# Softmax sums moved between on-chip buffers in two halves per sequence, and normalisation on GpSimd, in a fused attention and mixture-of-experts kernel

## What is computed

```python
q = layernorm(x) @ Wq.T + bq            # 32 heads of 16
k = ctx @ Wk.T + bk; v = ctx @ Wv.T + bv    # 8 groups of 16
w = softmax(mask(q k^T / 4))            # [b, group, head in group, query, key]
out = (w @ v) -> [b, 256, 512]
x = x + tanh(g_xattn) * (out @ Wo.T + bo)
xt = layernorm(x)
scores = sigmoid(xt @ gate.T); top 2 of 8 experts, chosen with expert_bias
x = x + tanh(g_ffn) * (routed experts (bf16) + shared expert (f32))
```

## Time and profile before

| | |
|---|---|
| median of three runs | 863.16 us |
| profiled execution | 858.97 us |
| its span, first to last instruction | 856.9 us |
| PE busy | 693.1 us (81%) |
| DVE busy | 469.0 us (55%) |
| ACT busy | 291.4 us (34%) |
| POOL busy | 68.7 us (8%) |
| mean granted TensorE clock | 0.877 of full |

### The profile page before, as it was taken

One profiled execution on the slowest core, in us unless ns is written; L12 is line 12 of the kernel. 1 busy time (PEld: TensorE's weight loads), 2 busy tenths in 40 slices (PEclk: granted clock), 3 DMA queues, 4 the chain that ended last, 5 costly groups with the idle time before them and its releaser, 6 DMA issues. The chain is left out here.

```text
span 856.9 us, 14813 instructions
## 1 busy us (share of the span) xinstructions
PE 693.1 (81%) x4417; PEld 480.3 (56%) x4417; DVE 469.0 (55%) x1041; ACT 291.4 (34%) x601; POOL 68.7 (8%) x100
## 2 busy tenths in 40 slices
PE   0436999699599789869959969989637799999998
PEld 0335758477377568648737747657326344444443
DVE  4417665368458467555836846564223455555554
ACT  1121454244333344433524433443201333333332
POOL 7400001001001000100100100000102000000000
PEclk9965979789799989978979988859657899999999
DMA  4785464444535543553545462430236022222111
GB/s 149 171 228 103 109 159 125 80 103 138 113 97 119 130 100 102 147 86 85 155 81 119 118 129 49 103 84 26 90 74 111 25 62 62 62 62 62 49 48 50
DMA packets 65199, 84.84 MB, mean 99 GB/s; under 512 B 15176, under 2 KB 43664, under 8 KB 64912
## 3 DMA queue, kind: packets, MB, share of 16 engines
q1 hardware_dynamic: 61008, 77.58, 36.9%
q0 software_dynamic: 2304, 6.29, 3.9%
q10 hardware_dynamic: 1856, 0.57, 0.3%
HBM read 60.75 MB, written 29.70 MB: 106 GB/s over the span
## 5 line engine op out<-in xcount | busy, mean ns | idle before, releaser
L593 ACT ACTIVATE probs<-ps 128x512 f32<-128x512 f32 x256 | 147.2, 598 | 150.3 <-PE ps L936 149.9
L800 DVE TENSOR_REDUCE mx<-ps 128x2 f32<-128x512 f32 x256 | 172.6, 683 | 39.7 <-PE ps L917 39.3
L917 PE MATMUL ps<-kst,qst 65*128 65x256 f32 x512 | 127.9, 336 | 65.3 <-DVE mx L800 59.6
L917 PEld LDWEIGHTS ps<-kst,qst 65*128 65x128 f32 x512 | 96.4, 213 | 115.1 <-DVE mx L800 76.1
L1085 PE MATMUL ps_h<-w,q_sg 128*128 128x512 bf16 x512 | 132.8, 383 | 5.2 <-PEq L77 5.2
L936 PE MATMUL ps<-qst,kst 66*128 66x512 f32 x256 | 113.8, 447 | 2.3 <-ACT probs L593 1.1
L1136 DVE SCALAR_TENSOR_TENSOR hid<-ps_h,sc_in,up 128x256 bf16<-128x256 f32 x128 | 61.9, 484 | 87.1 <-ACT up L1126 86.1
L1126 ACT ACTIVATE up<-ps_h,sc_in 128x256 f32<-128x256 f32 x128 | 60.7, 475 | 120.1 <-PE ps_h L1085 120.1
L1085 PEld LDWEIGHTS ps_h<-w,q_sg 128*128 128x128 bf16 x512 | 49.9, 99 | 67.8 <-issue 10.5
L949 PE MATMUL psa<-probs,v_st 128*32 128x256 f32 x1024 | 77.9, 427 | 1.2 <-ACT probs L593 1.2
L1103 PE MATMUL ps_o<-probs,hidT 128*128 128x512 bf16 x256 | 76.2, 380 | 0.8 <-DVE hidT L1142 0.8
(11 more groups left out here) (126 smaller groups left out, 1071.7 us busy)
## 6 DMA issues: line engine op xcount, KB each, us to landing
qst<-q_d SPq DMA_DIRECT2D x96, 128.0 KB
q_d<-q_sg SPq DMA_DIRECT2D x32, 256.0 KB, 3.0
a_d<-a_sb SPq DMA_DIRECT2D x32, 256.0 KB, 2.2
x_n<-in_x SPq DMA_DIRECT2D x8, 512.0 KB, 4.0
c_raw<-in_ctxT SPq DMA_DIRECT2D x8, 512.0 KB, 3.4
w<-in_w13T POOLq DMA_DIRECT2D x8, 512.0 KB, 16.1
x<-in_x SPq DMA_DIRECT2D x8, 512.0 KB, 3.4
a_dn<-a_d SPq DMA_DIRECT2D x8, 512.0 KB
```

The costliest lines, as they stand in the source:

```text
L593: act.activation(probs[:, v % 8, :], ps2[v % 2][:, :, :].rearrange("p h q -> p (h q)"), ACT.Exp, scale=HD ** -0.5).then_inc(s_exp, 1)
L800: dve.tensor_reduce(mx[:, c % 2, 0:8 * NT].rearrange("p (h t) -> p h t", t=NT)[:, h:h + 2, w // 2], ps1[u % 2][:, :, :], AX_X, ALU.max)\
L917: last = pe.matmul(o[:, i, :], qst[0:ROW_MAX, c, h, t * P:t * P + P], kst[0:ROW_MAX, c, g % 2, :], start=(i == 0 or not masked), stop=not ...
```

## The change

Four things change for each sequence:

1. The sums no longer go through DRAM on their way to `den`. `move_sums(b, c)` copies the rows of a chunk's sums straight from `a_sb` to 32 rows of `den`, in two DMAs, just ahead of `store_a` of the same chunk (u = 24, 1, 8, 17).
2. Values, reciprocal and its store and load are done in two halves of two chunks each. Half 0: values loaded and reciprocal stored at u = 5 (DVE's reciprocal at u = 4), loaded back at u = 9. Half 1: values loaded at u = 20, DVE's reciprocal at u = 20, stored at u = 21, loaded back at u = 23, which is behind `load_stack(b+1, 0)`.
3. The multiplication and the low part move from DVE to POOL, in halves by chunk, 128x512 each (`normalise`, `low_values`). ACT's high copies are at u = 16 and 27. POOL's order becomes values 2, power, normalise 0, low 0, values 3, residual and bias, values of b+1, normalise 1, low 1, powers, values.
4. W0 waits for both halves of the low part.

```diff
-            def load_sums(b):
-                for i in range(2):
-                    ready((s_aw[i], b * 32 + 32))
-                sp.dma_start(den[:, :], a_d[b, :, HD, :]).then_inc(s_den, 16)
-                sp.dma_start(a_dn[:, :, :].rearrange("p c q -> p (c q)"), a_d[b, :, 0:HD, :]).then_inc(s_ar, 16)
...
+            def move_sums(b, c):
+                ready((s_aev, b * G + 2 * c + 2), (s_rd, b * 2 + c // 2 - 1))
+                for w in range(2):
+                    row = 32 * c + 16 * w
+                    sp.dma_start(den[row:row + 16, :], a_sb[HD:P:32, c % 2, w, :]).then_inc(s_den[c % 2], 16)
+
+            def load_values(b, h):
+                for i in range(2):
+                    ready((s_aw[i], b * 32 + 16 * h + 16))
+                ready((s_ln2, b * LN2))
+                sp.dma_start(a_dn[:, 2 * h:2 * h + 2, :].rearrange("p c q -> p (c q)"),
+                             a_d[b, :, 0:HD, 2 * L * h:2 * L * h + 2 * L]).then_inc(s_ar[h], 16)
+
+            def store_r(b, h):
+                ready((s_rd, b * 2 + h + 1))
+                for i in range(2):
+                    c = 2 * h + i
+                    sp.dma_start(r_d[b, h, :, L * i:L * i + L], rden[32 * c:32 * c + 32, :]).then_inc(s_rw, 16)
+
+            def load_r(b, h):
+                ready((s_rw, b * 64 + 32 * h + 32), (s_ln2, b * LN2))
+                sp.dma_start(f(a_lo[:, 2 * h:2 * h + 2, :].rearrange("p c q -> p (c q)")),
+                             r_d[b, h].unsqueeze(1).broadcast_to([G, HD, 2 * L])).then_inc(s_rr[h], 16)
...
                     if prev and u in (1, 8, 17):
-                        store_a(b - 1, {1: 1, 8: 2, 17: 3}[u])
+                        c = {1: 1, 8: 2, 17: 3}[u]
+                        move_sums(b - 1, c)
+                        store_a(b - 1, c)
...
-                    if u == 18 and prev:
-                        load_sums(b - 1)
+                    if prev and u in (5, 20):
+                        load_values(b - 1, u // 20)
+                    if prev and u in (5, 21):
+                        store_r(b - 1, u // 21)
+                    if prev and u in (9, 23):
+                        load_r(b - 1, u // 23)
...
-                    if u == 21 and prev:
-                        store_r(b - 1)
...
-                    if u == 22 and prev:
-                        load_r(b - 1)
...
                     if attn and u == 24:
+                        move_sums(b, 0)
                         store_a(b, 0)
...
+            def normalise(b, h):
+                pool.wait_ge(s_rr[h], b * 16 + 16)
+                pool.wait_ge(s_ar[h], b * 16 + 16)
+                half = a_dn[:, 2 * h:2 * h + 2, :]
+                pool.tensor_tensor(half, half, a_lo[:, 2 * h:2 * h + 2, :].bitcast(F32), ALU.mult).then_inc(s_an, 1)
+
+            def low_values(b, h):
+                pool.wait_ge(s_ahi, b * 2 + h + 1)
+                pool.tensor_tensor(a_lo[:, 2 * h:2 * h + 2, :], a_dn[:, 2 * h:2 * h + 2, :],
+                                   a_hi[:, 2 * h:2 * h + 2, :].bitcast(F32), ALU.subtract).then_inc(s_alo, 1)
...
+                if attn:
+                    values(b, 2, None)
                 if nxt:
                     deviation1(b + 1)
+                if prev:
+                    normalise(b - 1, 0)
+                    low_values(b - 1, 0)
                 if attn:
-                    values(b, 2, None)
+                    values(b, 3, None)
                 if prev:
                     residual_bias(b - 1)
-                if attn:
-                    values(b, 3, None)
                 if nxt:
                     values(b + 1, 0, idx)
                 if prev:
+                    normalise(b - 1, 1)
+                    low_values(b - 1, 1)
                     deviation2(b - 1, 0)
...
-                    if u in (27, 28) and prev:
-                        t = u - 27
-                        act.wait_ge(s_an, b * NT - NT + t + 1)
-                        act.activation(a_hi[:, :, t * P:t * P + P], a_dn[:, :, t * P:t * P + P], ACT.Copy)\
+                    if u in (16, 27) and prev:
+                        h = u // 27
+                        act.wait_ge(s_an, b * 2 - 2 + h + 1)
+                        act.activation(a_hi[:, 2 * h:2 * h + 2, :], a_dn[:, 2 * h:2 * h + 2, :], ACT.Copy)\
                             .then_inc(s_ahi, 1)
...
-                    if u == 21 and prev:
-                        dve.wait_ge(s_den, b * 16)
-                        dve.reciprocal(rden[:, :], den[:, :]).then_inc(s_rd, 1)
-                    if u in (26, 27) and prev:
...
+                    if u in (4, 20) and prev:
+                        h = u // 20
+                        for i in range(2):
+                            dve.wait_ge(s_den[i], b * 64 - 64 + 32 * h + 32)
+                        wait(dve, s_rw, b * 64 - 128 + 32 * h + 32)
+                        dve.reciprocal(rden[64 * h:64 * h + 64, :], den[64 * h:64 * h + 64, :]).then_inc(s_rd, 1)
...
-                    pe.wait_ge(s_alo, b * NT + k + 1)
+                    pe.wait_ge(s_alo, b * 2 + 2)
```

More of the change, by code:

```diff
@@ L91, in attention_phase @@
         a_d = dram("a_d", (B, G, 32, CH * L))
-        r_d = dram("r_d", (B, G, CH * L))
+        r_d = dram("r_d", (B, 2, G, 2 * L))
         def pair(name, cols):
@@ L206, in attention_phase @@
         s_aw = [sem(f"s_aw{i}") for i in range(2)]
-        s_den = sem("s_den")
+        s_den = [sem(f"s_den{i}") for i in range(2)]
         s_rd = sem("s_rd")
         s_rw = sem("s_rw")
-        s_rr = sem("s_rr")
-        s_ar = sem("s_ar")
+        s_rr = [sem(f"s_rr{h}") for h in range(2)]
+        s_ar = [sem(f"s_ar{h}") for h in range(2)]
         s_an = sem("s_an")
@@ L348, in store_a @@
                              a_sb[:, c % 2]).then_inc(s_aw[c % 2], 16)
-            def load_sums(b):
-                for i in range(2):
-                    ready((s_aw[i], b * 32 + 32))
-                sp.dma_start(den[:, :], a_d[b, :, HD, :]).then_inc(s_den, 16)
-                sp.dma_start(a_dn[:, :, :].rearrange("p c q -> p (c q)"), a_d[b, :, 0:HD, :]).then_inc(s_ar, 16)
-            def store_r(b):
-                ready((s_rd, b + 1))
-                sp.dma_start(r_d[b], rden[:, :]).then_inc(s_rw, 16)
-            def load_r(b):
-                ready((s_rw, b * 16 + 16))
-                sp.dma_start(f(a_lo[:, :, :].rearrange("p c q -> p (c q)")),
-                             r_d[b].unsqueeze(1).broadcast_to([G, HD, CH * L])).then_inc(s_rr, 16)
+            def move_sums(b, c):
[4 more added lines that the diff above has]
+            def load_values(b, h):
+                for i in range(2):
+                    ready((s_aw[i], b * 32 + 16 * h + 16))
[11 more added lines that the diff above has]
+                             r_d[b, h].unsqueeze(1).broadcast_to([G, HD, 2 * L])).then_inc(s_rr[h], 16)
             def load_residual(b):
@@ L449, in _ @@
             passes(sp, body, prepare)
-            for s, n in ((s_kw, 16 * B), (s_rw, 16 * B),
+            for s, n in ((s_kw, 16 * B), (s_rw, 64 * B),
                          (s_qw[0], 32 * B), (s_qw[1], 32 * B), (s_aw[0], 32 * B), (s_aw[1], 32 * B)):
@@ L598, in values_out @@
                 wait(act, s_aw[(g // 2) % 2], b * 32 + 16 * (g // 4))
+                wait(act, s_den[(g // 2) % 2], b * 64 + 32 * (g // 4))
                 act.activation(a_sb[:, (g // 2) % 2, g % 2, :], psa[g % 2][:, 0:L], ACT.Copy).then_inc(s_aev, 1)
@@ L807, in body @@
                         norm1(b + 1, u - 9)
-                    if u == 21 and prev:
-                        dve.wait_ge(s_den, b * 16)
-                        dve.reciprocal(rden[:, :], den[:, :]).then_inc(s_rd, 1)
-                    if u in (26, 27) and prev:
-                        t = u - 26
-                        if t == 0:
-                            dve.wait_ge(s_rr, b * 16)
-                            dve.wait_ge(s_ar, b * 16)
-                        half = a_dn[:, :, t * P:t * P + P]
-                        dve.tensor_tensor(half, half, a_lo[:, :, t * P:t * P + P].bitcast(F32), ALU.mult)\
-                            .then_inc(s_an, 1)
-                    if u in (28, 29) and prev:
-                        t = u - 28
-                        dve.wait_ge(s_ahi, b * NT - NT + t + 1)
-                        dve.tensor_tensor(a_lo[:, :, t * P:t * P + P], a_dn[:, :, t * P:t * P + P],
-                                          a_hi[:, :, t * P:t * P + P].bitcast(F32), ALU.subtract).then_inc(s_alo, 1)
+                    if u in (4, 20) and prev:
[4 more added lines that the diff above has]
+                        dve.reciprocal(rden[64 * h:64 * h + 64, :], den[64 * h:64 * h + 64, :]).then_inc(s_rd, 1)
                     if u in (6, 7) and old:
```

## The result

The changed kernel takes 839.24 us (median of 4 runs, 837.31 to 840.51); the kernel before took 864.78 us beside it (4 runs). The ratio is 0.971, with a 95% interval of 0.967 to 0.975. Forecast were 837 us, a range of 809 to 858, and faster with a chance of 0.80. The profiled execution has a span of 836.8 us, 20.1 less than before. When the changed kernel was run once more beside the last three kernels, its six times lay between 824.6 and 840.7, and only the two lowest (824.6 and 831.1) counted as fast runs: by those two its ratio is 0.961 (0.954 to 0.968), by the medians of all six it is 0.971.

A forecast was written before the change was run, and what follows sets the result against it. The late load of reciprocals, stopping DVE, PE and ACT, was taken as the bound. Gains of 6 x 3.0 + 4 (pass 7) + 3.3 (pass 8) = 25.3 us gave 833.7 profiled, 837 us as median; range 809 to 858.

The forecast's parts named there:

- What bounds the kernel: Attention phase: one late load of reciprocals stops DVE (67.8 us in 8 places), PE and ACT, with half clock after.
- Sums and reciprocal: Sums copied directly to `den` by two DMAs of 0.6 us each; reciprocal ends at 424.3 instead of 426.5.
- Store of the reciprocals and issue of the load: Two stores of 0.34 us, then the stack's seven DMAs; load issued at 430.2, 0.6 us earlier than before.
- Its duration: Reciprocals' load, issue to use: 4.5 us instead of 9.7, from half the bytes and no stack behind; bounds 2.2 and 6.8.
- Chain on POOL and ACT: Multiplication, high part and low part up to W0: 3.4 us, against 3.1 on DVE.
- Clock: Slow stretch around W0 stays at 437.1 to 447.3, so a pass gains 3.0 of W0's 5.5 us.
- What I cost at nothing: Twelve more DMA issues per pass, some 6 us on SP, taken as covered; otherwise up to 1.2 us a pass.
- POOL against DVE: POOL's operations stretch DVE's two-SBUF-input ones; the change moves where, taken as zero for passes 1 to 6.
- Pass 8: Last pass, without attention: load at 623.3 instead of 624.47, W0 at 631.2, 3.3 us earlier.
- The clock stays full: Rival: the 3.9 us stop before W0 is too short to drop the clock; median 810 us; chance 0.14.
- The load is hardly faster: Rival: reciprocals' load stays at 6.8 us, median 849, or at 9.7, median 860; chance 0.25, of which 0.09 for 860.
- POOL holds up DVE: Rival: POOL's four new operations per pass delay DVE, costing 7 us a pass hit; median 880 us; chance 0.11.

The follow-up runs named there:

- e1_dve: The changed kernel with the multiplication and low part back on DVE, halves and data path kept; 833.01 us, ratio 0.965.
- e2_pool_only: The kernel before with only the multiplication and low part moved to POOL, still one 512 KB load of the reciprocals; 867.2 us, ratio 1.005.
- e9_sums_dram: The changed kernel with the sums going through DRAM again, in halves, and the second reciprocal and its store later; 852.17 us, ratio 0.989.
- e7_twice: The changed kernel with a second 256 KB load, into DRAM, ahead of the second half's load of reciprocals, POOL waiting for both; 854.55 us, ratio 0.994.
- e3_load_first: The changed kernel with the second load of reciprocals at unit 22, ahead of the next stack's seven DMAs; 831.32 us, ratio 0.962.
- e10_later: e8_best with W0 and W1 one unit later and the second half's multiplication, copy and low part two units later; 823.02 us, ratio 0.956.
- e4_row_first: The changed kernel with the row of maxima of unit 17 issued ahead of the sums' DMAs and store_a; 838.93 us, ratio 0.972.
- e6_half_all: The changed kernel with W0 and W1 using the first half twice, and the second half's copy and POOL work moved away from W0; 796.59 us, ratio 0.926.
- e8_best: The changed kernel with arithmetic on DVE, row of maxima first, reciprocals' store ahead of the values' load, reciprocals' load ahead of the stack; 831.47 us, ratio 0.967.

## Why the prediction was right, point by point

In short: the chain was right, and the forecast of 837 us for a measured 839 is closer than its parts. The sum said 25.3 us less for the profiled execution; it was 20.2. The median fell by 25.5, because the profiled execution of the kernel before was 0.5% short and the new one was not. That agreement is luck.

**What bounds the kernel.** Right. The load of the reciprocals stopped DVE, and with it PE and ACT. e1_dve and e2_pool_only show that it is the load, not the engine that waits for it.

**Sums and reciprocal.** Right to 0.1 us: the two issues took 1.24 (forecast 1.2), the reciprocal ended 5.4 us after the common event (5.3). Without it, in e9_sums_dram, 15 us of the 25 are gone, but that run has a later reciprocal too. e7_twice loses 15 us as well, so the shares don't simply add, and which part is the largest isn't shown.

**Store of the reciprocals and issue of the load.** The mis-sized term. I took 0.34 for each of the two stores, the row of the old one, and they take 1.64 for both. The load of values stands in front of them besides, up to 415.48. The load of the reciprocals was issued 13.2 us after the event instead of 11.2, later than in the kernel before (11.8), not 0.6 earlier. The old row was one DMA of the full 128 partitions; the new ones write 32 partitions into a strided block.

**Its duration.** 3.8 us, forecast 4.5 with bounds of 2.2 and 6.8. The rule was to halve what lies above a fixed part of 2.2. Pass 7 fell from 6.8 to 3.6, more than that; doubling in e7_twice gave 5.2, less. The step "the stack is no longer behind it" was right for the duration: with the stack behind it the same bytes take 5.3 (e3_load_first) or 7.4 us (e10_later). But I had not weighed it against the issue. Being behind the stack makes the load be issued 3.0 us later and saves 1.5, so the place that the change gave it costs 1.5 us a pass.

**Chain on POOL and ACT.** 3.3 us, forecast 3.4; POOL's operation took 1.26 to 1.30 us for the 1.2 that half of 2.38 gives.

**Clock.** The gain per pass came out at 3.1 for a forecast of 3.0, but by errors that cancel; this too is luck. W0 started 1.2 us later than forecast, and the slow stretch around it was 6.8 us and not 10.2. In pass 5, W1 ended 4.0 us earlier than before (437.95 less 409.26 is 28.7; 451.63 less 418.98 is 32.7). What is missing from 4.0 to 3.1 went elsewhere. The one place that recurs is between units 12 and 16, 3.8 us over passes 2 to 7. There ACT waits for the store of k in passes 2 to 6, 14.0 us in all (26.2 less the 12.2 of the start). The store is issued 0.7 us behind the last operation on k, little later than before (0.3), but it takes 4.1 us to land in the median and not 2.0. Just ahead of it stands the residual's load, by 0.7 us; before it was 3.9. That load waits for the stores of y, which land in 3.3 us instead of 2.1 and now follow the first half's load of reciprocals. This is the likely chain, but no run isolates it: e9_sums_dram, with the same load at unit 9, has only one such wait behind the start. I had named the row of maxima and the q stores as what stands behind the new DMAs, but not this one.

**What I cost at nothing.** The row of maxima in pass 7 was late by 2.67 us, so the cover I named was thin in the pass with the shortest units; e4_row_first shows that cutting this to 1.09 gives nothing. ACT's wait for the q buffer came too: 22.0 us in 12 places, 1.4 to 2.8 each, where it was 5.5 in 3. Pass 7 brought 1.1 us instead of 4, and its slow stretch of 20.5 us stayed. Passes 0 and 1 up to unit 16, which I had left out, lost 2.0.

**POOL against DVE.** Right in kind. The sum, forecast as zero, wasn't measured by itself, since e1_dve takes away both the holds and POOL's longer path. In passes 2 to 6 of the changed kernel one routing operation per pass is held for 1.28 or 1.29 us, the length of `low_values`; before it was up to 2.4 us, the length of the addition. The Trainium skill, "GPSIMD Engine Reference" (section 8), names DVE instructions with two SBUF inputs as those that contend with POOL; the held ones here all have two. DVE's maxima, which read PSUM, took their usual 0.7 us beside the 2.4 us addition. During `normalise` 1 and `low_values` 1 DVE ran nothing in pass 5, so nothing could be held there.

**Pass 8.** 2.9 us, forecast 3.3.

**The rivals.** *The clock stays full* did not come, and not only because the stop was 5.7 us and not 3.9: e10_later has stops of 3.9 to 4.6 us, and the clock falls in each. With no stop at all it stays full behind W0 (e6_half_all), so the rival had the right effect and the wrong length. *The load is hardly faster* did not come either, 3.8 us and not 6.8. *POOL holds up DVE*: the holds are in the trace, 1.3 us each, and the kernel got faster all the same. That the moved work would be worth nothing by itself (e2_pool_only, 1.005) was not among my rivals, and it is the main thing that the study adds.

## What to carry to other kernels

Ask of a wait that stops several engines what makes it late, before asking which engine should stand in it. Here the move to an idle engine alone made the kernel 0.5% slower, and with the rest it gained nothing, while a shorter way for a few small rows and half the bytes at the end of the chain brought the whole gain.

When a load that is waited for shares a queue with a bulky one, weigh both orders from a common event to its first use. Here it was issued 3.0 us earlier in front of the stack, took 1.5 us longer there, and was still in use 1.5 us sooner. Read the issue time of a DMA from a row of its own shape.

When a stop can't be shortened, let the engines come to it later. One more unit of scores for PE and two for DVE and ACT gave the best kernel.

## What was not expected of the hardware

- Two stores of 32 partitions each, 8 KB, into rows of a larger block took 0.82 us of SP's time apiece; one store of 128 partitions, 32 KB, took 0.34.
- The reciprocals' load of 256 KB took 3.6 to 4.4 us from issue to use with no stack behind it (changed kernel, all passes), 5.3 to 6.4 with the stack's 480 KB issued right behind it (e3_load_first), and 7.0 to 8.1 when a load of 256 KB also stood 1.6 us or less ahead (e8_best, e10_later).
- With PE's stops taken away, the granted clock stayed full behind W0 in passes 1 to 6. But it still fell to 1.2 GHz (0.52 over 10 us) behind 5.79 us of work in 6 and a stop of 0.99 us.
